# Expert stage of an attention and mixture-of-experts layer: the up-projection computed transposed from a fixed buffer, and the output stores in two alternating chains

## The reference, cut to what matters

```python
scores = jax.nn.softmax(xf @ w_gate, axis=-1)
weights, idx = jax.lax.top_k(scores, TOP_K)          # TOP_K = 2 of 8 experts
...
h = jnp.einsum('ecd,edf->ecf', exp_x, c_fc)          # 256 -> 768
a, g = jnp.split(h, 2, axis=-1)
h = jax.nn.silu(a) * g                               # 384
exp_out = jnp.einsum('ecf,efd->ecd', h, c_proj)      # 384 -> 256
...
return out.reshape(B, T, d)                          # each row: the sum of its two experts' rows times weights
```

## Time and profile before

| | us |
|---|---|
| median of 3 runs (lowest to highest) | 487.96 (487.74 to 491.83) |
| the profiled execution | 487.79 |
| its span in the trace | 486.0 |
| first and last output store (start) | 290.38 and 477.09 |
| TensorE busy, of the span | 389.5 (80%) |
| GpSimd, VectorE, ScalarE busy | 177.6, 262.5, 171.9 |

### The profile page before, as it was taken

The page is one execution under the profiler, slowest core; times in us unless marked ns, Lnnn a source line. Parts: engine busy times, 40 slices in busy tenths (PEclk is TensorE's granted clock), DMA queues, the critical chain, the costliest instruction groups (busy, mean ns, idle before and its releaser), DMA issues.

```text
span 486.0 us, 8302 instructions
## 1 busy us (share of the span) xinstructions
PE 389.5 (80%) x2218; PEld 257.8 (53%) x2219; DVE 262.5 (54%) x684; ACT 171.9 (35%) x336; POOL 177.6 (37%) x179
## 2 busy tenths in 40 slices
PE   0647798996969979695868799679999999999970
PEld 0524455664645656453535466457666566656640
DVE  3638566686987969688687546223323232323220
ACT  1430638463654726453354252112221212121210
POOL 5542333322743717352213315213323232323231
PEclk9977889898988989798898689889999999999996
DMA  7499194938749193580405513533232333233420
GB/s 230 152 196 147 38 207 159 207 115 161 213 120 227 50 185 112 128 160 33 140 10 179 187 42 77 109 77 40 51 58 36 60 43 57 43 57 44 61 44 4
DMA packets 65430, 51.75 MB, mean 106 GB/s; under 512 B 11880, under 2 KB 62328, under 8 KB 65400
## 3 DMA queue, kind: packets, MB, share of 16 engines
q1 hardware_dynamic: 57224, 42.36, 38.0%
q0 software_dynamic: 7008, 8.43, 10.3%
q10 hardware_dynamic: 1168, 0.59, 0.5%
HBM read 32.89 MB, written 19.06 MB: 107 GB/s over the span
## 4 chain that ended last, share of the span: by engine, by line
DMA 31%; DVE 25%; PE 24%; issue 10%; SPq 4%; ACT 2%; POOL 1%; ACTq 1%; POOLq 1%; DVEq 0%
DMA out<-CTt,GG 26%; DVE NEG L1043 7%; PE bank L803 5%; PE bank L769 4%; PE bank L868 3%; PE bank L839 3%; PE bank L852 2%; PE bank L776 2%; DVE bn L1001 2%; PE bank L918 2%; DVE AVT L1062 2%; DMA wf<-qparts_d 1%; DVE AVN L1065 1%; DVE ON L1070 1%; DVE R L1079 1%
## 5 line engine op out<-in xcount | busy, mean ns | idle before, releaser
L918 PE MATMUL bank<-wf,XN 128*128 x304 | 108.1, 498 | 1.6 <-DVE CTt L1268 1.0
L571 POOL DMA_INDIRECT out<-CTt,GG x38 | 58.9, 1551 | 133.5 <-DMA out<-CTt,GG 108.5
L1043 DVE TENSOR_REDUCE NEG<-bank 128x2 f32<-128x512 f32 x128 | 83.4, 682 | 42.0 <-PE bank L839 41.2
L670 ACT ACTIVATE PR<-bank 128x512 f32<-128x512 f32 x128 | 73.0, 593 | 80.1 <-PE bank L852 68.6
L918 PEld LDWEIGHTS bank<-wf,XN 128*128 128x128 f32 x304 | 55.5, 194 | 34.7 <-issue 8.2
L839 PE MATMUL bank<-KS,wf 99*128 99x256 bf16 x256 | 52.0, 288 | 22.4 <-DVE NEG L1043 15.1
L1261 DVE TENSOR_TENSOR QF<-bank,KF 128x384 f32<-128x384 f32 x38 | 21.2, 557 | 73.3 <-PE bank L918 72.7
L711 ACT ACTIVATE XTt<-bank 128x384 f32<-128x384 f32 x38 | 18.7, 492 | 117.0 <-PE bank L931 117.0
L938 PE MATMUL bank<-wp,XTt 128*128 x228 | 58.3, 394 | 0.7 <-ACT XTt L711 0.7
L852 PE MATMUL bank<-wf,KS 102*128 102x256 bf16 x256 | 49.7, 278 | 6.0 <-ACT PR L670 5.6
L521 POOL DMA_INDIRECT slots<-R,slot x32 | 32.5, 1015 | 43.6 <-DVE slot L1146 32.0
(11 more groups left out here) (160 smaller groups left out, 503.3 us busy)
## 6 DMA issues: line engine op xcount, KB each, us to landing
wf<-in_L_ffn_c_fc SPq DMA_DIRECT2D x8, 768.0 KB, 6.2
XG<-slots SPq DMA_DIRECT2D x40, 128.0 KB, 2.7
kparts_d<-KP SPq DMA_DIRECT2D x8, 384.0 KB, 2.5
qparts_d<-QP SPq DMA_DIRECT2D x8, 384.0 KB, 2.6
KS<-kparts_d SPq DMA_DIRECT2D x8, 384.0 KB
KS<-kparts_d SPq DMA_DIRECT2D x24, 128.0 KB
wf<-qparts_d SPq DMA_DIRECT2D x8, 384.0 KB
wf<-qparts_d SPq DMA_DIRECT2D x24, 128.0 KB
```

Of the source, the lines that this page charges most:

```text
L571: pool.indirect_dma_start(out_rows, bass.IndirectOffsetOnAxis(ap=GG[:, u, 1:2].bitcast(U32), axis=0), Y[:, u, :], None, bounds_check=last_ ...
L670: act.activation(PR[:, s % NPROB, :], STB[s % 2][:], ACT.Exp).then_inc(exp_done, 1)
L918: ins = pe.matmul(bank[2 + 2 * u + g][:, 0:FF], XTG[:, u, k, :], wf[:, bass.ds(off + (k * 2 + g) * FF, FF)], start=k == 0, stop=k == KC - 1)
L1043: dve.tensor_reduce(NEG[:, n % 2, t, 2 * hp:2 * hp + 2], MXB[m % 2][:].rearrange("p (i s) -> p i s", i=2), AX.X, ALU.max, negate=True).the ...
```

## The change

Five things change together.

1. `hidden` is computed transposed. The weights are now the stationary operand, in tiles of 128 x 128, and the rows the moving one: twelve matmuls of 128 columns in place of four of 384. The hidden values come out with their index on the partitions, so the product `HM` can be the stationary operand of `down` directly. `turn_hidden` and `hidden_copy` are gone.
2. The stationary operand is read from a fixed buffer `UP[u]`, laid over parts of `KS`. ScalarE copies the 1536 columns of a block's up weights there from `wf` (`copy_up`), two blocks ahead.
3. `down` writes to `bank[1]` for both parities, and so waits for `weigh` of the block before. On VectorE `rows_copy` of the next block now comes ahead of `gated`.
4. The semaphore `added` becomes two, by parity. A store waits for the store two blocks back, and for the store just before it only if the expert changes between them; a fourth row of `table` holds what the store waits for on the other chain. The first eight blocks keep waiting for the block before, and block 8, the first of the rest, is always treated as a change.
5. SyncE issues the gates of block t-3 behind the rows of block t (before: those of t-2), and reads its table entries ahead of its waits.

```diff
+        UP = [KS[:, i].rearrange("p h s -> p (h s)").bitcast(F32)[:, 0:KC * 2 * FF] for i in (2, 0)]
...
             def load_gates(t, u):
-                if later(t, 2):
-                    sp.wait_ge(added, (t - 1) * 16)
                 row = sp.value_load(table[0:1, 0, bass.ds(t, 1)], min_val=0, max_val=XROWS - P)
+                if later(t, 2):
+                    sp.wait_ge(added[u], (t - u) * 8)
...
                     load_block(2 * i + PEELED + 2 + u, u)
-                    load_gates(2 * i + PEELED + u, u)
+                    load_gates(2 * i + PEELED - 1 + u, 1 - u)
...
             def add_block(t, u):
+                if isinstance(t, int):
+                    others = (t + 1) // 2 * 16
+                else:
+                    others = pool.value_load(table[0:1, 3, bass.ds(t, 1)], min_val=16, max_val=16 * MAXPAIR)
                 pool.wait_ge(ys_ready, t + 1)
+                if later(t, 2):
+                    pool.wait_ge(added[u], (t - u) * 8)
                 if later(t, 1):
-                    pool.wait_ge(added, t * 16)
+                    pool.wait_ge(added[1 - u], others)
...
+            def copy_up(t, u):
+                if later(t, 2):
+                    act.wait_ge(h_ready, t - 1)
+                act.reg_load(up_at, table[0:1, 1, bass.ds(t, 1)])
+                off = act.snap(up_at, min_val=0, max_val=(E - 1) * KC * 2 * FF)
+                act.activation(UP[u][:], wf[:, bass.ds(off, KC * 2 * FF)], ACT.Copy).then_inc(up_ready, 1)
...
             def hidden(t, u):
+                pe.wait_ge(up_ready, t + 1)
                 pe.wait_ge(txe_ready, t + 1)
                 if later(t, 2):
                     pe.wait_ge(hm_ready, t - 1)
                 for g in range(2):
-                    for k in range(KC):
-                        ins = pe.matmul(bank[2 + 2 * u + g][:, 0:FF], XTG[:, u, k, :],
-                                        wf[:, bass.ds(off + (k * 2 + g) * FF, FF)],
-                                        start=k == 0, stop=k == KC - 1)
+                    for c in range(FC):
+                        for k in range(KC):
+                            ins = pe.matmul(bank[2 + 2 * u + g][:, c * P:(c + 1) * P],
+                                            UP[u][:, (k * 2 + g) * FF + c * P:(k * 2 + g) * FF + (c + 1) * P], XTG[:, u, k, :],
+                                            start=k == 0, stop=k == KC - 1)
...
+            def down(t, u):
+                off = at(down_at[u], (E - 1) * FC * D)
                 pe.wait_ge(hm_ready, t + 1)
                 if later(t, 1):
-                    pe.wait_ge(hte_ready, t)
+                    pe.wait_ge(ys_ready, t)
                 for c in range(FC):
-                    ins = pe.matmul(bank[3 + 2 * u][:, 0:D], HT[:, u, c, :], wp[:, bass.ds(off + c * D, D)],
+                    ins = pe.matmul(bank[1][:, 0:D], HM[:, u, c * P:(c + 1) * P], wp[:, bass.ds(off + c * D, D)],
                                     start=c == 0, stop=c == FC - 1)
...
             def step(t, u):
-                turn_hidden(t - 1, 1 - u)
                 hidden(t, u)
                 turn_rows(t + 1, 1 - u)
                 down(t - 1, 1 - u)
+                load_down_at(t, u)
...
+                if extra is not None:
+                    link(dve.memset(btmp2[:, 0:1], 0.0))
+                    link(dve.tensor_tensor(btmp2[:, 1:n], bcl[:, 1:n], bcl[:, 0:n - 1], ALU.is_equal))
+                    link(dve.scalar_tensor_tensor(out=table[:, 3, first:first + n], in0=btmp2[:, 0:n], scalar=-16.0, in1=other16[:],
+                                                  op0=ALU.mult, op1=ALU.add))
```

More of the change, by code:

```diff
@@ L458, in _ @@
                     load_block(2 * i + PEELED + 2 + u, u)
-                    load_gates(2 * i + PEELED + u, u)
+                    load_gates(2 * i + PEELED - 1 + u, 1 - u)
+            load_gates(last, 1)
             sp.wait_ge(out_stored[0], 16 * KNOWN)
@@ L585, in _ @@
                     add_block(2 * i + PEELED + u, u)
-            pool.wait_ge(added, pairs * 32)
+            for u in range(2):
+                pool.wait_ge(added[u], pairs * 16)
         @block.scalar
@@ L705, in silu @@
                 act.activation(SG[:, u, :], bank[2 + 2 * u][:, 0:FF], ACT.Silu).then_inc(sg_ready, 1)
-            def hidden_copy(t, u):
-                act.wait_ge(ht_ready, t + 1)
-                if later(t, 2):
-                    act.wait_ge(y_ready, t - 1)
-                act.activation(HT[:, u].rearrange("p c t -> p (c t)"), bank[1][:, 0:FF], ACT.Copy).then_inc(hte_ready, 1)
-            def step(t, u):
-                hidden_copy(t - 1, 1 - u)
-                silu(t, u)
+            act.wait_ge(ahead_ready, 1)
+            act.wait_ge(st_ready, UNITS * B)
+            act.wait_ge(we_in, 32 * E)
+            copy_up(0, 0)
+            copy_up(1, 1)
             silu(0, 0)
@@ L719, in _ @@
             copy_rows(B - 1)
-            hidden_copy(0, 0)
+            copy_up(2, 0)
             router_exponentials(B - 1)
             silu(1, 1)
+            copy_up(3, 1)
             for t in range(2, PEELED):
-                step(t, t % 2)
-            act.wait_ge(table_ready, 1)
+                silu(t, t % 2)
+                if t + 2 == AHEAD:
+                    act.wait_ge(table_ready, 1)
+                copy_up(t + 2, t % 2)
             pairs = act.value_load(npairs[0:1, 0:1], min_val=8, max_val=MAXPAIR)
-            last = act.value_load(npairs[0:1, 1:2], min_val=14, max_val=2 * MAXPAIR - 2) + 1
             with act.Fori(0, pairs - PEELED // 2) as i:
                 for u in range(2):
-                    step(2 * i + PEELED + u, u)
-            hidden_copy(last, 1)
+                    silu(2 * i + PEELED + u, u)
+                    copy_up(2 * i + PEELED + 2 + u, u)
         @block.tensor
@@ L914, in hidden @@
                 for g in range(2):
-                    if g == 1 and later(t, 2):
-                        pe.wait_ge(ys_ready, t - 1)
-                    for k in range(KC):
-                        ins = pe.matmul(bank[2 + 2 * u + g][:, 0:FF], XTG[:, u, k, :],
-                                        wf[:, bass.ds(off + (k * 2 + g) * FF, FF)],
-                                        start=k == 0, stop=k == KC - 1)
+                    for c in range(FC):
[3 more added lines that the diff above has]
+                                            start=k == 0, stop=k == KC - 1)
                     ins.then_inc(h_ready if g else ha_ready, 1)
-                load_up_at(t + 1)
-                load_down_at(t, u)
-            def turn_hidden(t, u):
+            def down(t, u):
+                off = at(down_at[u], (E - 1) * FC * D)
                 pe.wait_ge(hm_ready, t + 1)
                 if later(t, 1):
-                    pe.wait_ge(hte_ready, t)
+                    pe.wait_ge(ys_ready, t)
                 for c in range(FC):
-                    ins = pe.transpose(bank[1][:, c * P:(c + 1) * P], HM[:, u, c * P:(c + 1) * P], ident[:])
-                ins.then_inc(ht_ready, 1)
-            def down(t, u):
-                off = at(down_at[u], (E - 1) * FC * D)
-                pe.wait_ge(hte_ready, t + 1)
-                for c in range(FC):
-                    ins = pe.matmul(bank[3 + 2 * u][:, 0:D], HT[:, u, c, :], wp[:, bass.ds(off + c * D, D)],
+                    ins = pe.matmul(bank[1][:, 0:D], HM[:, u, c * P:(c + 1) * P], wp[:, bass.ds(off + c * D, D)],
                                     start=c == 0, stop=c == FC - 1)
@@ L961, in _ @@
             misc("X2", B - 1)
-            turn_hidden(0, 0)
             misc("LG", B - 1)
@@ L966, in _ @@
             down(0, 0)
-            turn_hidden(1, 1)
+            load_down_at(1, 1)
             misc("PF", B - 1)
@@ L972, in _ @@
             down(1, 1)
+            load_down_at(2, 0)
             for t in range(3, PEELED):
@@ L980, in _ @@
                     step(2 * i + PEELED + u, u)
-            turn_hidden(last, 1)
             down(last, 1)
```

43 lines of the change are left out of this document (21 added, 22 removed).

## The result

The changed kernel took 465.49 us (median of 4 runs, 464.91 to 468.68), the kernel before on the same chip 488.08 (4 runs, 487.74 to 491.83). The ratio is 0.953, 95% interval 0.9485 to 0.9573: faster by 4.7%. Some executions are slow ones, at a lower granted clock, and while the medians here are of all runs, every ratio is of the fast runs alone (of the kernel before on the chip of e9 to e12 only 6 of 17), so it need not be the quotient of the medians beside it. The forecast was 462.0 in a range of 455 to 479. The profiled execution took 464.91, its span is 463.2, the mean granted clock 0.916.

The account below looks back on a forecast made before the run. The chain of output stores, 4.82 us a block, was taken as the bound, with TensorE's 4.43 close behind. TensorE's new 4.19 step would move the last store from 477.09 to 451.3: 487.8 - 25.8 = 462.0 us, range 455 to 479.

Parts of the forecast that it names:

- The pair and the step: TensorE's up-projection: 0.111 us per load and matmul pair with full overlap, 24 pairs, making a block's step 4.19 us.
- the rival: TensorE: loads and matmuls of equal length don't overlap; halfway 501 us, none 549; no or little overlap had chance 0.07.
- Two chains fall under TensorE's pace: Expert loop: stores of two chains need 7.25 us for two blocks, 3.6 each, under TensorE's 4.19.
- the chains stay one: Rival, expert loop: stores nearly always wait for the block before, 4.82 us a block, time 483.4; chance 0.04.
- SyncE's order: First eight blocks: earlier rows leave stores bound by their own chain, store 7 at 328.1 instead of 332.48, gain 4.4 us.
- When TensorE becomes the bound: Expert loop: stores catch up and TensorE binds from about block 16, whose `down` ends at 361.9 us.
- The exponential's 1.0: Start of stage: block 2's larger copy ahead of the router's last exponential delays store 1 by about 1 us, to 299.2.
- The covers: Loop: ScalarE's 2.5 of 4.19 us hidden; VectorE's order free; shared `bank[1]` free unless stores are late.
- GpSimd waits for VectorE, not for its DMA, except at 8 changes: Sign of being right, expert loop: GpSimd waits for its own stores only at the 8 changes of expert.
- 1.0 that was added for bubbles: Last store: 1.0 us added for bubbles and the lower clock after a stall, moving it from 450.3 to 451.3.
- the tail: End of loop: after block 36's `down` ends at 445.7 us, the last store starts at 450.3, before the bubbles allowance.

Follow-up runs that it names:

- e9: Kernel before with the gates of block t-3 issued behind the rows of block t, each table read still behind its wait: 485.76 us against 494.89, ratio 0.9869.
- e12: Kernel before with two store chains and SyncE's whole new order, so the changed kernel without the transposed up-projection: 478.16 us against 494.89, ratio 0.9749.
- e3: Changed kernel with the second half of the up-projection's sum left out (12 pairs a block, not 24): 463.01 us, ratio 0.9386 to the kernel before.
- e1: Changed kernel with every store of the loop made to wait for the store before it: 480.50 us against 490.96 for the kernel before, ratio 0.976.
- e8: Kernel before with SyncE's new order alone, table reads ahead of the waits included: 482.72 us against 493.49, ratio 0.9817.
- e4: Changed kernel with SyncE's pads earlier, two ahead of block 3's gates and none ahead of block 8's rows: 466.66 us, ratio 0.9493 to the kernel before.
- e7: Changed kernel with pads earlier and block 2's weight copy behind the router's exponential and block 1's silu: 465.55 us, ratio 0.949 to the kernel before.

## Why the prediction was right

- **The pair and the step: right.** Forecast 0.111 and 4.19, measured 0.111 and 4.19 to 4.20. The forecast took full overlap from `down`, whose matmuls are longer than their loads, and said that no row had two equal sides; from that row alone it was a bet. But the earlier trace rows has such a pair: a transpose loads 128 x 128 and moves 128 columns, at 0.11 a pair, though its load is recorded with 0.141 where the up-projection's has 0.192. That would have left less to the rival. The Trainium skill, "TensorE: Matmul & The Clock Gate", section "Back-to-back issue gap", has 81 ns for a pair where the matmul alone has 56. The trace disagrees for this kernel's float32 pairs of 128 columns: 0.111 a pair is the pitch of the transposes' 128 columns, without a surcharge.
- **Two chains fall under TensorE's pace: right in kind, the size off.** Forecast 7.25 for two blocks; e3 shows 7.8, and 3.85 a block with the changes. The margin under 4.19 was 0.34 a block; a store slower by some 0.7 would have made the chains the bound again.
- **One chain: its price was wrong.** The rival "the chains stay one" had 4.82 a block and 483.4, within 1%. e1 is that rival, and it is 2.4% faster than before, because one chain runs at 4.53 under the new order of SyncE.
- **SyncE's order: the step that failed.** "These go out near 300, those of block 8 some 6 us earlier than before, and the first eight stores are bound by their own chain alone: block 7 at 299.2 + 6 x 4.82 = 328.1 ... Gain 4.4." Store 7 started at 331.86, 3.8 late. Store 1 was at 299.66, late by 0.5 (R by 1.15); the other 3.3 lie between the two stores, 32.2 where the forecast had 28.9 and before has 34.2. Most of that is SyncE's queue, read from the chain in time and, for the row of L417, from its own timeline:

```profile
313.04 3.00 DMA slots<-pad_row
...
317.92 0.36 SPq L417
...
319.05 1.72 DMA GG<-slots
...
320.85 0.50 DVE CTt L1276
...
321.58 1.56 PE bank L941 x6
```

  The forecast gave no time to the last two pads and none to the gates of block 5. The pads were issued from 311.92 on, behind the gates of block 4, which themselves wait for a store; they landed at 316.04; then come three table reads, block 8's rows (317.92), a fourth read and only then the gates of block 5 (319.05). The gates hold up `weigh` of block 5 (320.85), and with it store 5 (322.12, forecast 318.5); since both parities share `bank[1]`, `down` of block 6 waits for that `weigh` (321.58), and block 8's up-projection stands behind it: 323.98. The forecast had said of `bank[1]` that it passes the stores' lateness on, and then charged it 0.5 in the loop and nothing in the first eight blocks. e4 and e7, which move the pads, agree: block 8's up-projection starts at R + 45.4 and R + 42.1 instead of R + 46.6. (The 45.4 holds what e4's slow block 1 cost.) From store 1 to store 7 they take 29.6 to 29.7, so 2.3 to 3.0 of the missing 3.3 go with the pads. With the pads where they are the order alone doesn't reach 28.9 either: e8 has 31.4. In the changed kernel 1.8 of the 4.4 were left, counted from R.
- **And what the order gives in the loop was not in the sum at all.** e8 shows 0.25 a block for one chain. It didn't disturb the forecast, since with two chains the bound is TensorE.
- **When TensorE becomes the bound: earlier than forecast.** I had it from block 16 on, `down` of block 16 ending at 361.9. It was gapless from the up-projection of block 8 on, 323.98, and ten steps of 4.19 later, at 365.9, `down` of block 16 ended, 4.0 later than forecast. The pace was right, the point from which it counts was late.
- **The exponential's 1.0: right where it stands, too much at the store.** The exponential follows R 0.93 later than before, but store 1 only 0.27 (22.27 against 22.00). What took up the rest was not followed.
- **The covers held.** ScalarE's copy takes 1.49 (bound 1.87) and ScalarE is busy 52.46 of 110; VectorE's order and `bank[1]` let `down` wait nowhere in the loop up to block 36. Neither was tried alone. The sign "GpSimd waits for VectorE, not for its DMA, except at 8 changes" holds by the times, though not by the names in the wait rows (above).

The sum: the last store 454.20 against 451.3, late by 2.9. The late front moved TensorE by 4.2 (the last full `down` ends at about 449.9, forecast 445.7); 1.0 that was added for bubbles was not needed, and the tail was 0.3 shorter. What follows the last store is 9.0 (forecast 8.9). 464.91 measured, 462.0 forecast, an error of 0.6%. That it is not 0.9% is luck: the unneeded 1.0 and the shorter tail hid 1.3 of the late front.

## What to carry to other kernels

When two bounds lie close together (here 4.82 of a chain of stores and 4.43 of TensorE), price both after the change, and don't expect the parts to add. Under the new order of SyncE the loop took 4.57 a block (e8); with the transposed form added it took 4.53 (e1), with the second chain added 4.36 (e12), with both 4.08. A queue that issues in order, with waits in it, is to be walked through instruction by instruction at the place where two kinds of work meet; there the forecast lost most. And the order of small loads beside an accumulating store is worth a try by itself: here it gave 1.8% of the time (e8) for no further work on any engine.

## What was not expected of the hardware

**The clock at the start of the stage differs between executions.** Block 1's up-projection, of e4 and then of e7, in the timeline and in the windows:

```profile
288.12 5.35 PE L933 MATMUL bank<-XN,KS 128*128 128x128 f32 x24
...
288.00:293.00 5.00, 5.00 (x25) 5.00 (x25) 2.10 (x15) 3.50 (x5) 0.00 (x0) 0.50 0.00 0
```

```profile
282.79 2.92 PE L933 MATMUL bank<-XN,KS 128*128 128x128 f32 x24
...
283.00:287.00 4.00, 4.00 (x32) 3.82 (x32) 2.97 (x17) 3.96 (x6) 0.00 (x0) 1.00 0.00 0
```

The same 24 pairs took 5.35 at a granted clock of 0.50 (1.2 GHz) and 2.92 at 1.00 (2.4 GHz), after the same instructions of TensorE. In e4 block 0's had run at the upper level (2.94), and the clock fell during the router's logits between the two blocks; in the changed kernel of the result block 0's ran at the lower level and block 1's at the upper. That is 2.4 us in a stage of 185, and with the spread of the part ahead of the stage (R from 275.4 to 282.9) it is why differences of 4 us in the stage drown in the whole time.

**A store's time goes with what SyncE issues beside it**: 5.12 or 4.54 from one store to the next in the kernel before, with 0.35 us between the moments of a load (e9 above). Why was not shown.
